# Placing tokens into expert buckets: where GpSimd issues the placements, a third tile table, and how early the first expert tiles start

## The chip, the core and the metric

The kernel runs on one NeuronCore of a Trainium2 chip. Five engines run their own instruction streams and meet only through semaphores: TensorE (PE in the rows), VectorE (DVE), ScalarE (ACT), GpSimd (POOL) and SyncE (SP, which here only issues DMAs). The metric is the device time of one execution in microseconds (us), lower is better. Before the change three runs gave a median of 1045.76 us (1042.63 to 1046.62).

## The reference

x is 16 x 256 x 256 float32, that is 4096 tokens of width 256, or 32 tiles of 128 tokens. The context is 16 x 120 x 256. Four layers follow each other, each with a layernorm in front and a residual behind:

```python
x = x + L0_xattn(layernorm(x), ctx, Wq, Wkv)      # 16 heads of 16
x = x + L0_ffn(layernorm(x), W1, b1, W2, b2, gate_W, shared_W, shared_b, gamma, beta)
x = x + L1_xattn(layernorm(x), ctx, ctx, mask, Wq, Wk, Wv)
x = x + L1_ffn(layernorm(x), weight, bias)        # values rounded to a 6 bit grid

# inside L0_ffn: 8 experts, each token goes to its best two
probs = softmax(flat @ gate_W); topk_w, topk_idx = top_k(probs, 2)
combine = one_hot(topk_idx) * (topk_w / topk_w.sum())
out = 0.5 * gelu(flat @ shared_W + shared_b)
for e in range(8):
    h = gelu(flat @ W1[e] + b1[e])                # 256 -> 1024
    out = out + combine[:, e:e+1] * (h @ W2[e] + b2[e])
out = layernorm(out) * gamma + beta
```

The kernel computes only the two chosen experts of each token. It has to sort tokens by expert for that, and this sorting is what the change is about.

## The kernel before

**Three phases.** `attention_phase` runs the first cross attention and, for every tile, the shared product and the gate's logits. `expert_phase` runs 71 tiles of 128 rows (64 full ones and up to 7 for the remainders of 8 experts); a tile belongs to one expert. `second_phase` does the last two layers; the change does not touch it.

**The order is written out by hand.** Each engine has a function per phase (`sync`, `gpsimd`, `tensor`, `vector`, `scalar`), and what stands first in it runs first. Nothing is reordered, so an instruction that waits holds everything behind it on its engine.

**Attention cycles.** The phase is a loop over 18 cycles b = -2..15, one context batch each, so two token tiles t = 2b and 2b+1. For a tile the vector engine subtracts the row maxima of the scores (`largest`, `less_max`), ScalarE takes exponents, TensorE turns and weighs them, and VectorE divides by the sums (`over_sums`, writes `a_x`). Then GpSimd adds the residual (`residual`, line 757), VectorE takes the statistics (`stats2`, line 1071), GpSimd forms the inverse deviation (`inverse_std2`) and VectorE normalises (`normalise2`). The residual is loaded by SP (`load_residual`, line 622) into `a_xres`, of which there are two; for the even tile it is issued behind two loads of expert weights (`w_sb`, 512 KB each). The key blocks `a_kbd` (`key_blocks`) come once a cycle on GpSimd, so their starts mark off the cycles in the trace.

**Routing.** The 32 tiles form four groups of eight. For a group VectorE picks two experts per token (`choose`, parts 0 to 7, with one exponent on ScalarE), TensorE counts ranks (`count`), and `places` computes each token's row in the buckets. GpSimd then writes token number and weight to that row in HBM: one indirect DMA (`put`, line 405) per tile and choice, 16 per group, 64 in all, 8 bytes per row. `table` computes for each expert tile which expert it has and where its bucket rows start; the first table covers 24 tiles (`EARLY_TILES`) and needs two groups, the second covers the other 47 and needs all four. Groups 0 and 1 are placed in attention cycles 9 to 15, groups 2 and 3 in expert tiles 2 to 5 and 6 to 9.

**Expert tiles.** SP fetches a tile's 128 bucket rows (`slots`, `b_slots`), GpSimd gathers the token rows by them (`gather`, line 1449, four buffers, so three tiles ahead), TensorE turns them (`turn_rows`, line 1504), ScalarE keeps them, TensorE does the first product (`first_product`, line 1515, into `b_H`), ScalarE the gelu, TensorE the second product (line 1527, into `b_Y`), VectorE adds the bias (`finish`, line 1616) and scales by the weight, and GpSimd adds the rows to HBM by an indirect accumulate (`scatter`, line 1460). VectorE also copies the tile's expert weights beforehand (`tile_weights`, `b_w`, line 1605, 1.23 us). In iteration n TensorE runs the first product of tile n+1, turns tile n+2 and runs the second product of tile n. GpSimd's iteration n gathers tile n+3 and then places and scatters; the first scatter is at n = 9. The functions in `starts` let the attention phase begin the first tiles. `gelu_chunk` and `store_chunk` bring the shared part into the accumulator in 16 chunks, all of which must be stored before the first scatter.

## Time and profile before

| | us |
|---|---|
| median of three runs (range) | 1045.76 (1042.63 to 1046.62) |
| the profiled execution's own time | 1037.06 |
| its span in the profile | 1035.3 |
| attention, up to the last attention product that TensorE runs without a gap | about 308 |
| expert tiles, first `b_xT` to last `b_Y` | 317.7 to 866 |
| busy: PE / DVE / ACT / POOL | 946.8 / 529.4 / 509.2 / 515.6 |
| indirect DMAs on POOL: 64 placements, 71 gathers, 71 scatters | 68.1, 75.7, 141.8 busy |

The profiled execution is shorter than the median of the timed runs by 8.7 us; sums over its rows stand against 1037.06. In the page's picture of 40 slices PE is at nine tenths from slice 17 to slice 33, which is most of the expert phase, and between six and nine tenths before. The chain of work that ended last is PE for 44% of the span, nearly all of it the two expert products; "issue" is time in which an engine waited for nothing that the profile shows.

### The profile page before, as it was taken

To read this page: it belongs to the slowest core of one execution; us is meant where nothing else is said; L and a number is where in the kernel's file an instruction comes from. 1 tells how busy PE (TensorE), PEld (TensorE's weight loads), DVE (VectorE), ACT (ScalarE), POOL (GpSimd) and SP (SyncE) were. 2 spreads that over 40 slices of the span, in tenths; PEclk is the share of its full clock that TensorE was granted. 3 is DMA by queue.
4 is the path that set the end of the run, shared out by engine and by line. 5 is a ranking of instruction groups with operands and counts; after the bars stand their busy time and mean duration, and the time that the engine had idled before them with its cause. 6 is when DMAs were issued, how large, how long until landed. Compare 5 with 4: busy or idle time off the path is not lost.

```text
span 1035.3 us, 22010 instructions
## 1 busy us (share of the span) xinstructions
PE 946.8 (91%) x7131; PEld 808.0 (78%) x7131; DVE 529.4 (51%) x1276; ACT 509.2 (49%) x1292; POOL 515.6 (50%) x675
## 2 busy tenths in 40 slices
PE   6999999989876887999999999999999999798776
PEld 4767777666646777899999999999999998676654
DVE  4677898877762332443323232232323223899871
ACT  4776777766643442334333333333333333577663
POOL 2524343655643075656444443434444442688873
PEclk9999999999998998999999999999999999999897
DMA  4264454655643455434322212222121227333210
GB/s 142 81 167 158 133 167 125 154 123 138 158 113 92 151 113 107 36 55 59 51 38 41 37 31 37 34 39 39 34 42 31 42 40 192 111 92 98 86 42 31
DMA packets 90734, 89.58 MB, mean 87 GB/s; under 512 B 19808, under 2 KB 85792, under 8 KB 90496
## 3 DMA queue, kind: packets, MB, share of 16 engines
q1 hardware_dynamic: 74944, 69.48, 23.6%
q0 software_dynamic: 15680, 18.69, 12.3%
q8 instruction: 62, 1.02, 0.5%
q14 instruction: 48, 0.39, 0.2%
HBM read 56.74 MB, written 31.39 MB: 85 GB/s over the span
## 4 chain that ended last, share of the span: by engine, by line
PE 44%; DVE 7%; issue 5%; DMA 3%; POOL 3%; ACT 2%; POOLq 0%; SPq 0%; DVEq 0%; ACTq 0%
PE b_H L1515 20%; PE b_Y L1527 20%; DMA ffn_rows<-b_y,b_slots 2%; POOL buckets L405 2%; DVE c_x_bn L1975 2%; PE c_f_ps L2227 1%; PE b_xT L1504 1%; ACT c_probs L2142 1%; DVE c_centred L1988 1%; ACT c_xn L2097 1%; DVE c_x L2065 1%; DVE c_amax L2045 1%; POOL b_rows L1449 1%; DVE c_nmax L2036 1%; DMA c_ctx<-in_ctx 0%
## 5 line engine op out<-in xcount | busy, mean ns | idle before, releaser
L1684 ACT ACTIVATE b_hiddenT<-b_H,b_b 128x128 f32<-128x128 f32 x568 | 162.5, 369 | 325.5 <-PE b_H L1515 325.5
L1515 PEld LDWEIGHTS b_H<-b_rowsT,b_w 128*128 128x128 f32 x2272 | 266.6, 193 | 4.8 <-ACT b_rowsT L1691 1.1
L1515 PE MATMUL b_H<-b_rowsT,b_w 128*128 128x128 f32 x2272 | 267.4, 276 | 0.5 <-ACT b_rowsT L1691 0.4
L1527 PE MATMUL b_Y<-w_sb,b_hiddenT 128*128 x1136 | 263.0, 386 | 0.0
L1460 POOL DMA_INDIRECT ffn_rows<-b_y,b_slots x71 | 141.8, 1998 | 216.0 <-DVE b_y L1620 141.9
L1527 PEld LDWEIGHTS b_Y<-w_sb,b_hiddenT 128*128 128x128 f32 x1136 | 214.9, 194 | 27.5
L1616 DVE TENSOR_TENSOR b_y<-b_Y,b_b 128x256 f32<-128x256 f32 x71 | 30.1, 425 | 329.9 <-PE b_Y L1527 320.6
L1605 DVE COPY b_w<-w_sb 128x2048 f32 x71 | 87.6, 1234 | 32.2 <-issue 26.0
L1206 ACT COPY a_probsT<-a_T 120x512 f32<-120x512 f32 x128 | 74.9, 585 | 46.6 <-PE a_T L911 40.7
L1449 POOL DMA_INDIRECT b_rows<-xn_rows,b_slots x71 | 75.7, 1066 | 43.2 <-issue 20.8
L405 POOL DMA_INDIRECT buckets<-r_pay,r_place x64 | 68.1, 1064 | 53.9 <-DVE r_place L398 28.6
L911 PE MATMUL a_T<-ident,a_probs 128*120 128x128 f32 x512 | 79.0, 283 | 17.0 <-ACT a_probs L1198 17.0
L911 PEld LDWEIGHTS a_T<-ident,a_probs 128*120 128x120 f32 x512 | 57.3, 140 | 31.6 <-ACT a_probs L1198 20.6
L1198 ACT ACTIVATE a_probs<-a_probs 128x960 f32<-128x960 f32 x64 | 64.3, 1005 | 32.1 <-DVE a_probs L1049 30.8
L757 POOL TENSOR_TENSOR a_x<-a_x,a_xres 128x256 f32<-128x256 f32 x32 | 23.6, 739 | 112.7 <-DMA a_xres<-in_x 57.4
L1041 DVE TENSOR_REDUCE a_max<-a_S 128x8 f32<-128x960 f32 x64 | 73.3, 1146 | 8.9 <-PE a_S L891 8.8
L1049 DVE TENSOR_TENSOR a_probs<-a_S,a_max 128x960 f32<-128x960 f32 x64 | 73.2, 1144 | 0.9 <-issue 0.2
L925 PE MATMUL a_O<-a_probsT,a_vaug 120*32 120x128 f32 x1024 | 54.6, 286 | 0.5 <-ACT a_probsT L1206 0.3
L1504 PE MATMUL b_xT<-ident,b_rows 128*128 128x128 f32 x142 | 28.1, 281 | 20.9 <-DMA b_rows<-xn_rows,b_slots 20.9
L925 PEld LDWEIGHTS a_O<-a_probsT,a_vaug 120*32 120x32 f32 x1024 | 20.2, 108 | 29.4 <-issue 23.0
L2227 PE MATMUL c_f_ps<-c_wdT,c_xdT 128*128 128x256 f32 x128 | 37.7, 448 | 1.4 <-ACT c_xdT L2168 1.4
L1691 ACT COPY b_rowsT<-b_xT 128x256 f32<-128x256 f32 x71 | 27.6, 388 | 21.3 <-PE b_xT L1504 21.3
(222 smaller groups left out, 1315.8 us busy)
## 6 DMA issues: line engine op xcount, KB each, us to landing
w_sb<-in_L_ffn_W SPq DMA_DIRECT2D x32, 512.0 KB, 4.1
a_xin<-in_x SPq DMA_DIRECT2D x16, 256.0 KB, 3.1
a_xres<-in_x SPq DMA_DIRECT2D x32, 128.0 KB, 4.7
x_rows<-a_x SPq DMA_DIRECT2D x32, 128.0 KB, 1.7
xn_rows<-a_xn SPq DMA_DIRECT2D x32, 128.0 KB, 2.7
shared_rows<-a_shared SPq DMA_DIRECT2D x32, 128.0 KB, 2.8
b_spare<-shared_rows SPq DMA_DIRECT2D x16, 256.0 KB, 4.7
ffn_rows<-b_spare SPq DMA_DIRECT2D x16, 256.0 KB, 3.7
```

Of the source, the lines that this page charges most:

```text
L405: pool.indirect_dma_start(bucket_d, IndirectOffsetOnAxis(place[:, t, k:k + 1], 0), pay[:, t, k, :], None).then_inc(s_put[g // 2], 16)
L911: i = pe.transpose(T_ps[q % 2][0:CTX, j * P:(j + 1) * P], pr[q // 2][:, 4 * (q % 2) + j, :], ident[:])
L925: i = pe.matmul(O_ps[VB * j:VB * (j + 1), q * P:(q + 1) * P], vaug[t // 2 % 2][0:CTX, 4 * q + j, :], pT[q % 2][0:CTX, j, :], start=True, s ...
L1041: dve.tensor_reduce(mx[h][:].rearrange("p (r j) -> p r j", r=RG), scores_of(h), AX.X, ALU.max).then_inc(s_mx, 1)
L1049: dve.tensor_tensor(pr[h][:].rearrange("p (r j) c -> p r j c", r=RG), scores_of(h), mx[h][:].rearrange("p (r j) -> p r j", r=RG).unsqueeze ...
L1206: act.copy(pT[q % 2][0:CTX].rearrange("p j n -> p (j n)"), T_ps[q % 2][0:CTX, :]).then_inc(s_T, 1)
L1449: pool.indirect_dma_start(xg[n % AHEAD][:], None, xn2_d, IndirectOffsetOnAxis(iw[:].bitcast(I32)[:, n, 0:1], 0)).then_inc(s_x[n % AHEAD], 16)
L1460: pool.indirect_dma_start(acc_d, IndirectOffsetOnAxis(iw[:].bitcast(I32)[:, n, 0:1], 0), y[n % KEPT_Y][:], None, bounds_check=TOK + SPARE - 1,
L1515: j = pe.matmul(H_ps[i][:, c * P:(c + 1) * P], w1c[i][:, k * HID + c * P:k * HID + (c + 1) * P], xT[:, k * P:(k + 1) * P], start=(k == 0), ...
L1527: j = pe.matmul(y_ps[i][:, 0:D], hT[i][:, c * P:(c + 1) * P], w2_sb[:, bass.ds(e * (HB * D) + c * D, D)], start=(c == 0), stop=(c == HB - 1))
L1605: dve.tensor_copy(w1c[i][:], w1_sb[:, bass.ds(e * (KC * HID), KC * HID)])
L1684: j = act.activation(hT[i][:, c * P:(c + 1) * P], H_ps[i][:, c * P:(c + 1) * P], ACT.Gelu, bias=b1c[i][:, c:c + 1])
```

## The change

It moves instructions in all five streams. Its core, shortened:

```diff
+FIRST_TILES = 9
+    RANGES = ((0, FIRST_TILES), (FIRST_TILES, EARLY_TILES), (EARLY_TILES, SLOT_TILES))
 # GpSimd, attention cycles
-    put_some(b, 1, 1, 2)      # one or two placements at four points of a cycle
...
             for b in CYCLES:
                 t = 2 * b
                 residual(t - 2)
                 add_beta(t - 3)
                 inverse_std2(t - 2)
+                if b == B - 1:
+                    starts["gather"](pool, 0)
+                put_some(b, 3)
+                if 1 <= b < 5:
+                    routing.constants(pool, b - 1)
                 residual(t - 1)
                 add_beta(t - 2)
                 inverse_std2(t - 1)
                 key_blocks(b + 1)
                 inverse_std1(b + 2)
+                put_some(b, 1 if b < FIRST_PUT + 4 else 3 if b == B - 1 else 2)
 # put
+        if g % 2 == 1 and (t % GT, k) == (0, 0):
+            pool.wait_ge(s_put[g // 2], 16 * 2 * GT)
 # SyncE, attention cycles
-                if b == 2:
-                    routing.fill_buckets(sp)
+                if 4 <= b < 7:
+                    routing.fill_buckets(sp, b - 4)
...
-            starts["slots"](sp, 0)
+                if b == B - 2:
+                    starts["slots"](sp, 0)
+                if b == B - 1:
+                    starts["load_b2"](sp)
+                    starts["slots"](sp, 1)
             load_residual(TILES - 1)
-            starts["slots"](sp, 1)
 # TensorE, end of the attention phase
+                if b == B - 1:
+                    starts["rows"](pe, 0)
                 turn_probs(t + 1, 2)
...
             weigh(t, 2)
+            starts["first"](pe, 0, 0)
             weigh(t, 3)
             shared_gate(t - 2)
+            starts["first"](pe, 0, 1)
             pe.wait_ge(s_oT, TILES)
             turn_back(t)
-            starts["rows"](pe, 0)
             turn_xn2(t - 1)
-            starts["first"](pe, 0, 0)
+            starts["rows"](pe, 1)
             shared_gate(t - 1)
-            starts["first"](pe, 0, 1)
-            starts["rows"](pe, 1)
+            starts["first"](pe, 1, 0)
+            starts["first"](pe, 1, 1)
+            starts["rows"](pe, 2)
             turn_xn2(t)
-            starts["first"](pe, 1, 0)
+            starts["second"](pe, 0)
             shared_gate(t)
-            starts["first"](pe, 1, 1)
 # VectorE, end of the attention phase
                 less_max(t + 1, 1)
+                if b == B - 1:
+                    starts["weights"](dve, 0)
                 keep_shared(t - 2)
...
             normalise2(t - 1)
-            starts["weights"](dve, 0)
             over_sums(t)
             stats2(t)
+            starts["weights"](dve, 1)
             keep_shared(t - 1)
-            starts["weights"](dve, 1)
             normalise2(t)
+            routing.table(dve, 1, 3)
+            starts["weights"](dve, 2)
             keep_shared(t)
+            starts["finish"](dve, 0)
 # expert phase
-        CONST_AT = 10
+        CONST_AT = 11
-        COUNT_AT = {1: THIRD, 5: LAST}
-        PUT_AT = {2: THIRD, 6: LAST}
-        TABLE_AT = 7
+        COUNT_AT = {5: THIRD, 9: LAST}
+        PLACE_AT = {5: THIRD, 9: LAST}
+        PUT_AT = {6: THIRD, 10: LAST}
+        TABLE_AT = 10
+        EXTRA_ADD = 16
-                return 0 if n < FIRST_ADD else 2 if (n - FIRST_ADD) % 4 == 0 else 1
+                return 0 if n < FIRST_ADD else 2 if n >= EXTRA_ADD and n % 4 == 0 else 1
-            for s, value in past["attention"] + past["rows_stored"]:
-                sp.wait_ge(s, value)
-            sp.dma_start(b2_bc[:], b2.rearrange("e d -> (e d)").partition_broadcast(P)
-                         ).then_inc(s_b12, 16)
```

In words: the first 16 placements of tokens (group 0) alone now decide a first table of nine tiles, the next 15 tiles get a table from groups 0 and 1, and the last 47 one from all groups. The attention phase now contains the whole of tile 0 and the first products of tile 1. The second bias (`b2`, 1 MB once it is broadcast over the partitions) is loaded in the last attention cycle and has memory of its own there. Groups 2 and 3 are chosen and counted later, and placed at tiles 6 to 9 and 10 to 13. GpSimd's constants are made in four parts in cycles 1 to 4 instead of at once in cycle 1, and the initial filling of buckets, spare rows and accumulator is issued in cycles 4, 5 and 6 instead of in cycle 2. The turned rows of tiles 0 and 1 go to a part of `b_H`'s memory.

GpSimd's stream in attention cycle 13 before. L757 is `residual`, L766 `add_beta`, L405 a placement, L747 and L750 `inverse_std2`, L775 `key_blocks`, L735 to L741 `inverse_std1`:

```order
L757 TENSOR_TENSOR a_x_0<-a_x_0,a_xres 128x256
L766 TENSOR_TENSOR a_x_1<-a_x_1,a_beta 128x256
L405 DMA buckets<-r_pay,r_place 32896x2
L747 TENSOR_SCALAR a_var_eps<-a_mv 128x1
L750 TENSOR_TENSOR a_rstd<-a_var_eps,a_minus_half 128x1
L757 TENSOR_TENSOR a_x_1<-a_x_1,a_xres 128x256
L766 TENSOR_TENSOR a_x_0<-a_x_0,a_beta 128x256
L405 DMA buckets<-r_pay,r_place 32896x2 x2
```

The same stretch of the same cycle in the changed kernel, where the lines are 781, 790, 420, 771 and 774:

```order
L781 TENSOR_TENSOR a_x_0<-a_x_0,a_xres 128x256
L790 TENSOR_TENSOR a_x_1<-a_x_1,a_beta 128x256
L771 TENSOR_SCALAR a_var_eps<-a_mv 128x1
L774 TENSOR_TENSOR a_rstd<-a_var_eps,a_minus_half 128x1
L420 DMA buckets<-r_pay,r_place 32896x2 x3
L781 TENSOR_TENSOR a_x_1<-a_x_1,a_xres 128x256
L790 TENSOR_TENSOR a_x_0<-a_x_0,a_beta 128x256
```

The placement that stood ahead of `inverse_std2` now stands behind it with two more, between the even tile's residual and the odd tile's; those behind the odd tile's go to the cycle's end.

GpSimd in attention cycle 15, changed kernel (before, no gather stood in the cycle; the first one came behind the residual of tile 30). L1489 is the gather:

```order
L771 TENSOR_SCALAR a_var_eps<-a_mv 128x1
L774 TENSOR_TENSOR a_rstd<-a_var_eps,a_minus_half 128x1
L1489 DMA b_rows<-xn_rows,b_slots 128x256
L420 DMA buckets<-r_pay,r_place 32896x2 x3
L781 TENSOR_TENSOR a_x_1<-a_x_1,a_xres 128x256
```

The gather of tile 0, which waits for its bucket rows (`b_slots`), now stands ahead of the residual of tile 29.

SyncE at the turn from cycle 14 to cycle 15, before. L1394 loads a chunk, L622 a residual, L629 stores `a_x`, L650 loads expert weights:

```order
L1394 DMA b_spare<-shared_rows 128x2x256
L622 DMA a_xres<-in_x 128x256
L629 DMA x_rows<-a_x_0 128x256
L650 DMA w_sb<-in_L_ffn_W 128x1024
```

and in the changed kernel, where four tiles' bucket rows (L1408 reads a row number, L1409 issues the load; one of the four is shown) stand in between:

```order
L1436 DMA b_spare<-shared_rows 128x2x256
L1408 TENSOR_LOAD r_tile_row
L1408 ISA x2
L1409 ISA
L1409 DMA b_slots<-buckets 128x2
```

Behind the fourth of these comes the residual load of tile 29, which before followed the chunk's load directly.

## Rows read from the trace of the kernel before

**Rows 1.** Windows: stretch, length, busy of PE, PEld, DVE, ACT, POOL; clock, DMA.

```profile
440.60:855.90 415.30, 415.30 (x2865) 391.55 (x2864) 124.18 (x237) 146.43 (x515) 187.59 (x120) 1.00 0.26 42
335.33:440.60 105.27, 88.88 (x579) 81.58 (x578) 37.99 (x113) 39.13 (x116) 53.88 (x46) 0.92 0.49 100
164.49:281.50 117.01, 107.38 (x1073) 78.05 (x1072) 91.83 (x208) 79.96 (x141) 67.70 (x110) 0.99 0.56 141
113.52:146.97 33.45, 33.45 (x349) 25.12 (x348) 30.07 (x67) 26.19 (x48) 13.82 (x29) 1.00 0.46 149
41.04:79.19 38.15, 35.65 (x353) 25.54 (x353) 27.11 (x54) 26.15 (x46) 17.61 (x48) 1.00 0.55 157
```

**Rows 2.** Waits of DVE, 113.52 to 146.97: total us, times, longest.

```profile
DVE a_bn L1071 <- POOL a_x L757: 1.2, 2, 0.6
```

**Rows 3.** Waits of DVE, 164.49 to 281.50.

```profile
DVE a_bn L1071 <- POOL a_x L757: 19.9, 8, 4.3
```

**Rows 4.** Timeline of POOL, cycle 13: start, us, line, what [idle before <-releaser].

```profile
243.99 1.07 POOL L405 DMA_INDIRECT buckets<-r_pay,r_place  x1 [0.56 <-issue]
246.72 0.72 POOL L757 TENSOR_TENSOR a_x<-a_x,a_xres 128x256 f32<-128x256 f32 x1 [1.66 <-DMA a_xres<-in_x]
255.87 0.73 POOL L757 TENSOR_TENSOR a_x<-a_x,a_xres 128x256 f32<-128x256 f32 x1 [5.64 <-DMA a_xres<-in_x]
```

**Rows 5.** Tile a_xres, 113.52 to 164.49: landing times of the residual loads.

```profile
DMA to landing us min/median/max: 2.6/3.6/5.0
```

**Rows 6.** Tile a_xres, 164.49 to 281.50: landing times.

```profile
DMA to landing us min/median/max: 3.3/5.1/7.4
```

**Rows 7.** Timeline of SP's DMA queue, 289 to 313 us.

```profile
290.40 0.49 SPq L622 DMA_DIRECT2D a_xres<-in_x  x1
...
308.94 3.69 SPq L1373 DMA_DIRECT2D b_slots<-buckets  x4
312.68 0.43 SPq L622 DMA_DIRECT2D a_xres<-in_x  x1
```

**Rows 8.** Timeline of POOL, 296 to 316 us.

```profile
296.88 0.72 POOL L757 TENSOR_TENSOR a_x<-a_x,a_xres 128x256 f32<-128x256 f32 x1 [5.58 <-DVE a_x L1062]
...
314.81 1.09 POOL L1449 DMA_INDIRECT b_rows<-xn_rows,b_slots  x1 [7.71 <-DMA b_slots<-buckets]
```

**Rows 9.** Timeline of PE, 317 to 409 us.

```profile
317.68 0.69 PE L1504 MATMUL b_xT<-ident,b_rows 128*128 128x128 f32 x2 [9.16 <-DMA b_rows<-xn_rows,b_slots]
...
335.33 3.73 PE L1515 MATMUL b_H<-b_rowsT,b_w 128*128 128x128 f32 x32
...
343.89 0.22 PE L381 MATMUL b_pre<-r_sel,r_before 128*128 128x72 bf16 x1 [4.61 <-DVE r_sel L353]
...
370.70 0.67 PE L1504 MATMUL b_xT<-ident,b_rows 128*128 128x128 f32 x2 [3.39 <-DMA b_rows<-xn_rows,b_slots]
...
408.09 0.69 PE L1504 MATMUL b_xT<-ident,b_rows 128*128 128x128 f32 x2 [5.65 <-DMA b_rows<-xn_rows,b_slots]
```

**Rows 10.** Timeline of POOL, 379 to 431 us.

```profile
379.60 1.83 POOL L405 DMA_INDIRECT buckets<-r_pay,r_place  x1 [0.30 <-issue]
...
395.39 1.81 POOL L405 DMA_INDIRECT buckets<-r_pay,r_place  x1 [7.98 <-DVE r_pay L358]
...
401.32 1.79 POOL L1449 DMA_INDIRECT b_rows<-xn_rows,b_slots  x1 [0.30 <-issue]
...
414.91 0.98 POOL L1449 DMA_INDIRECT b_rows<-xn_rows,b_slots  x1 [0.30 <-issue]
...
428.94 0.99 POOL L405 DMA_INDIRECT buckets<-r_pay,r_place  x1 [0.30 <-issue]
430.23 0.98 POOL L1449 DMA_INDIRECT b_rows<-xn_rows,b_slots  x1 [0.30 <-issue]
```

**Rows 11.** Waits of SP, 400 to 440 us.

```profile
SPq L1370 <- DMA buckets<-r_pay,r_place: 1.6, 1, 1.6
```

**Rows 12.** Timeline of DVE, 341 us.

```profile
341.44 0.42 DVE L1616 TENSOR_TENSOR b_y<-b_Y,b_b 128x256 f32<-128x256 f32 x1 [9.31 <-DMA b_b<-in_L_ffn_b]
```

322 lines of the change are left out of this document (175 added, 147 removed).

## The prediction

> **What bounds the kernel now.** I read the windows first [rows 1]. From 440.6 us on the expert phase is TensorE's alone: it is busy for the whole window, 57 tiles in 415.3 us, so 7.29 us a tile with the few extra products in it. That floor stays. The time is lost in front of it. The eleven tiles between 335.3 and 440.6 us took 105.3 us where 11 x 7.29 = 80.1 would do: 25.2 us lost, 16.4 of them idle TensorE (105.3 less 88.9 busy), the rest mostly a granted clock of 0.92, since TensorE falls back to its lower level, 1.2 of 2.4 GHz, after each gap. In the attention phase I took the stretches between key block operations as cycles. Cycles 6 and 7 take 16.7 us each (33.45 for two) with TensorE busy throughout; cycles 9 to 14, in which groups 0 and 1 are placed, take 117.0, 16.7 more than six times that.
>
> The views of waits say why. In the undisturbed cycles VectorE waits 1.2 us for the residual that GpSimd adds [rows 2], in the six others 19.9 us in eight waits [rows 3]. But GpSimd is not simply busy with placements: in cycle 13 one ends at 245.1 and the even tile's residual starts at 246.72, released by the residual's load, and the odd tile's waits for its load as well [rows 4]. These loads land after 3.6 us (median) without placements about [rows 5] and after 5.1, up to 7.4, with them [rows 6]. So a placement costs twice: 1.3 us of GpSimd (0.99 + 0.30), and slower transfers around it.
>
> The timeline of TensorE between 317 and 409 us gives the gaps in the expert phase [rows 9]: 9.2 us before the first tile (gather), 4.6 us for the third group's selection, 3.4 and 5.7 us for gathers. Behind the 4.6 stands VectorE, which had waited 9.3 us for the second bias [rows 12]. Behind the 5.7 stands GpSimd, which waited 8.0 us with a placement whose weights were not ready, while the gather queued behind it, issued at 401.3, reached TensorE at 408.1 [rows 10].
>
> **The change part by part.** Sums are over the profiled execution (1037.06 us for a span of 1035.3; 8.7 under the median of 1045.76) and are then taken off the median.
>
> *Constants and filling.* The two cycles from 41.0 to 79.2 us took 38.15 [rows 1], 4.7 over two undisturbed ones. In them GpSimd made its constants in one piece, and the filling of buckets and spare rows stood ahead of a residual load. In four parts behind `inverse_std2` the constants lie in an idle stretch of GpSimd; the filling still stands in SP's queue, now in three cycles. I take 1.5 us gained. Ends: 0 (each part costs what the whole did) and 4.7.
>
> *Placements in the attention cycles.* Their number stays: 4 in cycles 9 to 12 as before, then 5, 5 and 6 for 6, 6 and 4. Three now stand after `inverse_std2` of the even tile, ahead of a residual for which GpSimd waits 5.6 us anyway [rows 4]: 3 x 1.3 = 3.9 fits. The three that lay between the odd and the next even residual shrink to one (two in 13 and 14). The even residual then comes with the load, about 1.5 to 2.5 us sooner a cycle. The bill goes to the odd tile: its load is now in flight beside three placements, and if it lands after 5.1 rather than 3.6 it is late by up to 1.5. VectorE cannot go below the 16.7 us cycle. So 17.6 us for each of cycles 9 to 12 (before, 18.75 on average in them), 19.5 for 13 and 14, which also carry chunk loads and one new wait: the first placement of group 1 waits until all of group 0 have landed. How long a placement takes to land can be bounded: the last one started at 428.94, and SP waited 1.6 us for it [rows 11] from the table's end at 432.1, so 4.8 us. That is 4 x 17.6 + 2 x 19.5 = 109.4, 7.6 less than 117.0; I take 6, since in that count nothing goes wrong. Ends: a loss of 4 (odd tiles late by 1.5 and the even ones no sooner: 6 x 1.5 = 9 lost against 5 gained) and a gain of 14 (nearly all the excess).
>
> *Cycle 15 and the turn into the expert phase.* Here I expect no gain, against what three early tiles suggest. The bucket rows of tiles 0 to 3 are issued at the end of SP's cycle 14, where before the residual load stood at 290.4 [rows 7]. Four take 3.7 us, so until 294.1, and before the gather began 2.2 us after their last issue (312.63, 314.81 [rows 7, 8]): 296.3 now. GpSimd stands at that gather from about 289, and behind it are queued three placements and the residual of tile 29: 296.3 + 1.4 + 3.9 gives 301.6 instead of 296.9 [rows 8]. VectorE needs that residual before it can subtract the next maxima, so the last two tiles are 4.7 us late. VectorE's copy of tile 0's weights, 1.4 us with its bias, now stands ahead of the gate's read on which TensorE waits, and the first two halves of the first product (3.6 us) stand ahead of the last turns: TensorE ends the attention products near 318 rather than 308.5. SP then has the bias and five more rows, 0.4 + 4.6 us, ahead of the residual load of tile 31, which was issued at 312.7 [rows 7] and will be at about 317.5, landing 3.6 later, 321. Statistics and the weight copy of tile 1 follow: its first product starts at about 324.4. Two halves (3.9), two turns (0.8), the second product of tile 0 (3.5), a gate product (1.1) and 1.5 of low clock bring the next tile's first product to 335.2, as before (335.33 [rows 9]). The 9.2 us gap is filled and comes back as two smaller ones. I take 0. Ends: +5 (load of tile 31 hidden) and -5 (both delays longer).
>
> *Tiles 1 to 11.* The bias is there, so the 4.6 us gap goes, and no placement waits for weights in tiles 2 to 9, since groups 2 and 3 are chosen three tiles ahead of their placing. What is late next is GpSimd in tiles 6 to 13, where placements and scatters now lie together for five tiles (9 to 13) instead of one. Two iterations of four placements and a gather took 414.91 - 401.32 = 13.6 us [rows 10], 6.8 each, which fits into 7.29. A scatter is 2.0 us busy on average and 0.3 between: 9.15 an iteration. From the start of tile 6's iteration on TensorE: placements begin after VectorE's places, at 2.7, and end at 8.2; two iterations make 21.9; five with a scatter 67.7; and the first placement of group 3 waits for the landing of group 2's last, 4.8 less what lies between, 2.5 more: the gather of tile 17 is issued at 70.2. It lands after 2.9 (314.81 to 317.68 [rows 8, 9]) to 6.8 us (401.32 to 408.09); with 4.8, 75.0. TensorE wants it at 9 x 7.29 + 3.8 = 69.4. So 5.6 us late, and 2 for the low clock after a gap (8.8 us of excess over busy and idle time before, for four gaps): 7.5 lost. Gain 25.2 - 7.5 = 17.7. Ends: 25 (a scatter hides between placements and landings are short) and 9 (every iteration meets a weight copy).
>
> That last end rests on a row: placements and gathers that fall beside VectorE's weight copy took 1.8 us, three in the rows, others 0.98 [rows 10], 0.85 more. The Trainium skill (SBUF — State Buffer, "Who interferes with whom") says that a VectorE copy in its two-port mode takes the shared port pair for the whole instruction, and that GpSimd's descriptor writing is fully blocked meanwhile; so every tile would charge GpSimd up to the copy's length. The trace agrees in kind, with 0.85. The page's rule speaks against this change, as the copies come once a tile: at 0.85 in each of eight iterations, against one in two in the 6.8, it would be 3.4 us more lateness, and the forecast would be 1024.
>
> *Choosing, counting and tables later.* VectorE is busy 124 of 415 us in the expert phase [rows 1]; the 0.2 us steps and the third table hide there. If they did not, the cost were under 3 us. TensorE's counts are the same instructions.
>
> Sum: 1.5 + 6 + 0 + 17.7 = 25.2 us; 1037.1 - 25.2 = 1011.9, and of the median 1045.8 - 25.2 = 1020.6.
>
> **The rivals.** *B, all goes well*: attention cycles near their floor and GpSimd never late: 3 + 9 + 1 + 23 = 36, 1010. For it: 5.6 us idle before the odd residual. Against: slower landings beside placements.
>
> *C, the lateness moves*: the odd tile's load takes what the even one's gives, and tiles 12 to 15 wait longer for gathers: 0 + 0 + 0 + 12, 1034. For it: the odd residual too waited for its load in cycle 13 [rows 4].
>
> *D, the early tiles cost what the later ones give*: the delay in cycle 15 is twice mine (-9), tiles gain 12, attention nothing: 3 us, 1043. For it: five things queue behind one gather. Against: 25 us were lost before in a place that the change clears.
>
> *E, slower, one mechanism*: placements slow other transfers wherever they stand. The iteration of tile 9 before had four placements, a gather and two scatters and took 430.23 - 414.91 = 15.3 us [rows 10]. If the five iterations with one scatter take that, the gather of tile 17 starts at 21.9 + 76.5 = 98.4 and is 33.8 us late; with 2 of clock 35.8 are lost against 25.2 before, and the attention cycles gain nothing: 1045.8 - 1.5 + 10.6 = 1055. It decides for slower from about 14.5 us an iteration. Against: that iteration held the wait of the second scatter for the first, which one a tile does not have.
>
> **How the numbers follow.** Forecast 1020.5, own range 1014 to 1029, chance 0.50; B 0.15; C 0.20; D 0.09; E 0.06. A difference of 0.5%, 5.2 us, is about what a measurement of this kernel can tell from none. Faster by more holds the forecast, B, C and a little of D: 0.87; within it 0.08 (D); slower 0.05 (E, less its edge). The range 1010 to 1036 takes in B's and C's values and leaves out D and E and half of B's tail.
>
> **What would show it.** Right: cycles 9 to 14 together 105 to 114 us; VectorE's wait for the residual under 12 us there; in cycle 15 a wait of GpSimd for bucket rows at the first gather and VectorE idle 4 to 5 us behind it; no TensorE gap over 1 us in tiles 1 to 8; gaps for gathered rows between tiles 11 and 16, 4 to 8 us in sum. Wrong: residual waits unchanged in sum (C), a GpSimd iteration over 12 us in tiles 9 to 13 (E), TensorE's first product of tile 2 after 340 us on the new clock of the trace (D), or gaps in tiles 1 to 5, which I price at nothing.

## The result, and the profile after

| | before | changed | ratio, 95% interval |
|---|---|---|---|
| timed, median (range) | 1045.76 us (1042.63 to 1046.62) | 1027.98 us (1025.12 to 1036.61) | 0.9869 (0.9838 to 0.9899) |
| a second set of runs | 1046.08 us (1039.82 to 1048.64) | 1029.86 us (1024.37 to 1032.96) | 0.9849 (0.9793 to 0.9904) |
| profiled executions | 1037.06, 1040.56 us | 1036.61, 1027.53 us | |

The first row stands on five executions of each kernel, the second on seven of before and four of the changed one. A ratio leaves out executions that lie over 1.5% above the fastest of their kernel, which are three in experiment 7 and one in experiment 8. The change makes the kernel 14 to 18 us faster; 25.2 were forecast. The first profiled execution of before is shorter than all its timed ones and the first of the changed kernel is its longest, so this pair alone would show nothing (0.4 us). I therefore use two profiles of each, and the experiments' where they leave a stretch as it is. Below, *mark n* is the n-th start of a key block operation, counted from 0 (41.04 us of before is mark 2; what the prediction calls cycles 9 to 14 lies between marks 9 and 15), and *tile n* the start of tile n's first product. These stretches come from the traces' instruction starts.

| stretch, us | before | changed | forecast of the gain | gain of the means |
|---|---|---|---|---|
| start to mark 9 | 164.5, 163.4 | 159.7, 160.4 | 1.5 | 3.9 |
| mark 9 to 15 | 117.0, 115.2 | 117.8, 107.5 | 6 | 3.5 |
| mark 15 to tile 2 | 53.8, 52.3 | 61.5, 59.9 | 0 | -7.6 |
| tile 2 to 13 | 105.3, 118.9 | 98.7, 98.1 | 17.7, less what tiles 13 to 16 lose | 13.7 |
| tile 13 to 24 | 81.9, 81.9 | 87.8, 92.2 | (in the row above) | -8.1 |
| tile 24 to 70 | 333.3, 333.3 | 333.3, 333.3 | 0 | 0 |
| tile 70 to the end | 179.6, 173.9 | 176.1, 174.5 | 0 | 1.4 |

Rows two and three need care, for the change moved mark 15 itself. Before, two placements stood between the residual of tile 27 and the key blocks; now they stand behind. GpSimd, before and then changed (first profiles):

```profile
276.64 0.73 POOL L757 TENSOR_TENSOR a_x<-a_x,a_xres 128x256 f32<-128x256 f32 x1 [5.58 <-DMA a_xres<-in_x]
281.50 1.24 POOL L775 TENSOR_TENSOR a_kbd<-a_kT,a_head_mask 128x240 f32<-128x240 f32 x2
```

```profile
275.17 0.72 POOL L781 TENSOR_TENSOR a_x<-a_x,a_xres 128x256 f32<-128x256 f32 x1 [6.18 <-DMA a_xres<-in_x]
277.51 1.12 POOL L799 TENSOR_TENSOR a_kbd<-a_kT,a_head_mask 128x240 f32<-128x240 f32 x2
```

The mark follows that residual by 4.8 to 4.9 us in all profiles with the old placement points and by 2.3 to 2.5 in all with the new, so 2.4 us change rows without any time being won or lost (mark 9 has not moved). From the residual of tile 15 to that of tile 27 the kernel before took 114.6 and 112.8 us and the changed one 117.9 and 107.5, a gain of 1.0; from there to tile 2 it is 58.7 and 57.2 against 63.9 and 62.3, a loss of 5.2.

The windows of the changed kernel that answer to [rows 1] (length, busy time of PE, PEld, DVE, ACT and POOL, clock, DMA share, GB/s). First profile; the stretches are mark 9 to 15, tile 2 to 13 and tile 13 to 16:

```profile
159.73:277.51 117.78, 106.56 (x1068) 77.19 (x1066) 90.37 (x210) 77.97 (x139) 66.10 (x109) 0.99 0.49 135
339.04:437.70 98.66, 88.85 (x576) 81.48 (x575) 35.10 (x107) 41.58 (x120) 35.77 (x32) 0.91 0.41 98
437.70:466.90 29.20, 25.66 (x163) 21.94 (x161) 13.29 (x36) 8.52 (x29) 22.41 (x18) 1.00 0.41 38
```

Second profile, the same three:

```profile
160.35:267.90 107.55, 103.71 (x1056) 75.10 (x1054) 90.00 (x211) 78.19 (x139) 65.99 (x110) 1.00 0.52 148
327.80:425.90 98.10, 86.93 (x577) 80.36 (x575) 35.10 (x107) 41.90 (x120) 35.65 (x32) 0.91 0.42 99
425.90:459.70 33.80, 28.25 (x164) 23.51 (x163) 13.47 (x35) 8.63 (x29) 25.34 (x21) 0.95 0.38 40
```

In the attention cycles VectorE's wait for the residual, 19.9 us before [rows 3], and GpSimd's wait for the residual's input stand thus in the first profile:

```profile
DVE a_bn L1097 <- POOL a_x L781: 18.4, 10, 4.6
POOL a_x L781 <- DMA a_xres<-in_x: 30.9, 8, 6.5
```

and in the second:

```profile
DVE a_bn L1097 <- POOL a_x L781: 11.9, 9, 2.3
POOL a_x L781 <- DMA a_xres<-in_x: 14.5, 7, 3.9
```

The same instructions, once with half the waiting: the placements' order did not settle this. What did is not found.

Cycle 15, first profile. GpSimd, answering to [rows 8]:

```profile
296.80 1.08 POOL L1489 DMA_INDIRECT b_rows<-xn_rows,b_slots  x1 [9.34 <-DMA b_slots<-buckets]
...
301.78 0.73 POOL L781 TENSOR_TENSOR a_x<-a_x,a_xres 128x256 f32<-128x256 f32 x1
...
314.32 0.82 POOL L781 TENSOR_TENSOR a_x<-a_x,a_xres 128x256 f32<-128x256 f32 x1 [6.32 <-DVE a_x L1088]
...
325.59 0.72 POOL L781 TENSOR_TENSOR a_x<-a_x,a_xres 128x256 f32<-128x256 f32 x1 [7.54 <-DMA a_xres<-in_x]
```

SP's queue, answering to [rows 7]:

```profile
290.57 4.06 SPq L1409 DMA_DIRECT2D b_slots<-buckets  x4
294.67 0.43 SPq L643 DMA_DIRECT2D a_xres<-in_x  x1
...
303.59 0.43 SPq L671 DMA_DIRECT2D w_sb<-in_L_ffn_W  x1
...
317.24 0.39 SPq L1427 DMA_DIRECT2D b_b<-in_L_ffn_b  x1
318.48 4.77 SPq L1409 DMA_DIRECT2D b_slots<-buckets  x5
323.30 0.43 SPq L643 DMA_DIRECT2D a_xres<-in_x  x1
```

VectorE's copy of tile 0's weights:

```profile
310.47 1.23 DVE L1650 COPY b_w<-w_sb 128x2048 f32 x1 [3.97 <-issue]
```

and TensorE, answering to [rows 9]:

```profile
305.34 1.11 PE L934 MATMUL a_T<-ident,a_probs 128*120 128x128 f32 x4 [8.10 <-ACT a_probs L1226]
312.32 1.09 PE L960 MATMUL a_M<-ident,a_oT 128*128 128x128 f32 x4 [5.87 <-DVE logits L1122]
...
329.00 5.42 PE L1562 MATMUL b_H<-b_rowsT,b_w 128*128 128x128 f32 x32 [3.21 <-DVE b_b L1651]
...
339.04 3.73 PE L1562 MATMUL b_H<-b_rowsT,b_w 128*128 128x128 f32 x32
```

The gather at 296.80 and the residual at 301.78 were forecast at 296.3 and 301.6. But the prediction counted on the clock of the trace before. Counted from the residual of tile 27 (276.64 before, 275.17 here, 265.37 in the second profile), the residual of tile 29 was forecast at 25.0 us, and came at 26.6 and 24.9. The rest is worse than forecast: the input of tile 31 was to be asked for 15.9 us behind that residual and was asked for 21.5 and 21.7 us behind it.

The chain between the two is in the rows. The store of tile 28's `a_x` waits for GpSimd's work behind the late residual, and the last load of the first product's weights stands behind this store in SP's queue: issued at 303.6 (298.7 before). VectorE's copy of tile 0's weights waits in the code for all 16 of these loads (`s_w1`). The profile calls this wait of 3.97 us "issue", but the trace has the last landing at 309.4 and the copy at 310.5. The gate's read stands behind the copy, TensorE waits 5.87 us for it, GpSimd's residual of tile 30 waits 6.32 us for VectorE, and only then does SP come to its stores, the bias, the five slots and the input of tile 31. The second profile has the same wait, 4.14 us. Tile 1's first product starts at 329.0 instead of 324.4.

In the expert phase VectorE's 9.3 us wait for the second bias [rows 12] is gone:

```profile
340.07 0.42 DVE L1663 TENSOR_TENSOR b_y<-b_Y,b_b 128x256 f32<-128x256 f32 x1 [0.34 <-issue]
```

The 4.6 us gap for the selection and the gathers' gaps in tiles 1 to 7 are gone (tile 3 to 8 took 36.6 us in both profiles; 42.4 and 55.0 before). Then this happens, in both, at tile 9. TensorE, second profile:

```profile
380.92 4.90 PE L1562 MATMUL b_H<-b_rowsT,b_w 128*128 128x128 f32 x25 [2.00 <-issue]
386.95 0.39 PE L1562 MATMUL b_H<-b_rowsT,b_w 128*128 128x128 f32 x2 [1.13 <-issue]
387.68 0.27 PE L1562 MATMUL b_H<-b_rowsT,b_w 128*128 128x128 f32 x1 [0.34 <-issue]
389.10 0.57 PE L1562 MATMUL b_H<-b_rowsT,b_w 128*128 128x128 f32 x1 [1.15 <-issue]
391.22 0.37 PE L1562 MATMUL b_H<-b_rowsT,b_w 128*128 128x128 f32 x1 [1.55 <-issue]
393.36 0.37 PE L1562 MATMUL b_H<-b_rowsT,b_w 128*128 128x128 f32 x1 [1.77 <-issue]
...
396.23 0.37 PE L1551 MATMUL b_xT<-ident,b_rows 128*128 128x128 f32 x1 [1.76 <-issue]
```

GpSimd meanwhile, unhindered:

```profile
387.54 0.98 POOL L420 DMA_INDIRECT buckets<-r_pay,r_place  x1 [0.30 <-issue]
...
390.10 1.62 POOL L1500 DMA_INDIRECT ffn_rows<-b_y,b_slots  x1 [0.30 <-issue]
```

A product of 32 matmuls that takes 3.73 us elsewhere takes 13.5 (380.92 to 394.47). Most single matmuls last 0.27 to 0.39 us but start 0.7, 1.4 or 2.1 us apart, and no release is named ("issue"): in these rows TensorE waits for no other engine and for no data that the profile knows. Tile 8 to 13 took 54.8 and 54.3 us where the pitch gives 36.5. I call this the crawl. The granted clock is lower there: 0.91 over the window above.

The other engines stand too. In the first profile, where the same happens at tile 9:

```profile
386.65 3.62 PE L1583 MATMUL b_Y<-w_sb,b_hiddenT 128*128 x16
394.78 6.08 PE L1562 MATMUL b_H<-b_rowsT,b_w 128*128 128x128 f32 x25 [4.51 <-ACT b_rowsT L1739]
```

```profile
393.32 1.14 ACT L1732 ACTIVATE b_hiddenT<-b_H,b_b 128x128 f32<-128x128 f32 x4 [6.90 <-remote]
406.90 0.42 DVE L1663 TENSOR_TENSOR b_y<-b_Y,b_b 128x256 f32<-128x256 f32 x1 [19.35 <-remote]
```

By TensorE's row the second product ends at 390.3. The trace has the semaphore update that VectorE waits for at 406.8, 16.5 us later; in the second profile the corresponding update comes 14.4 us behind its row. One tile earlier both stand at 383.0. So the crawl is not only late starts of TensorE: results that its rows show as finished are signalled late.

### The profile page after: what moved, and what is told of

The parts are those of the page before. It is cut to its first block, busy times and chain, and to the rows that moved or that the text cites. A ratio compares the mean times of both kernels' runs of the same rounds, so it can differ in the third digit from the quotient of the medians.

```text
span 1034.9 us, 22048 instructions
## 1 busy us (share of the span) xinstructions
PE 944.5 (91%) x7131; PEld 805.1 (78%) x7131; DVE 532.5 (51%) x1300; ACT 509.8 (49%) x1294; POOL 512.5 (50%) x675
## 4 chain that ended last, share of the span: by engine, by line
PE 68%; DVE 9%; DMA 8%; issue 4%; ACT 4%; POOL 3%; SPq 3%; another core or an unknown queue 1%; DVEq 0%; POOLq 0%; ACTq 0%
PE b_H L1562 24%; PE b_Y L1583 23%; DMA a_xres<-in_x 4%; PE a_T L934 4%; PE a_O L889 3%; PE a_O L948 3%; PE a_S L914 2%; DVE c_x_bn L2023 2%; DMA ffn_rows<-b_y,b_slots 2%; PE b_xT L1551 1%; PE a_M L983 1%; ACT c_xn L2145 1%; ACT c_probs L2190 1%; DVE c_centred L2036 1%; PE a_M L960 1%
## 5 line engine op out<-in xcount | busy, mean ns | idle before, releaser
L1562 PEld LDWEIGHTS b_H<-b_rowsT,b_w 128*128 128x128 f32 x2272 | 269.6, 195 | 20.7 <-issue 10.1
L1562 PE MATMUL b_H<-b_rowsT,b_w 128*128 128x128 f32 x2272 | 272.2, 278 | 13.9 <-ACT b_rowsT L1739 6.0
L1583 PE MATMUL b_Y<-w_sb,b_hiddenT 128*128 x1136 | 260.3, 382 | 1.5 <-issue 1.3
L1583 PEld LDWEIGHTS b_Y<-w_sb,b_hiddenT 128*128 128x128 f32 x1136 | 212.1, 192 | 29.1 <-issue 2.8
L1500 POOL DMA_INDIRECT ffn_rows<-b_y,b_slots x71 | 137.6, 1938 | 190.1 <-DVE b_y L1667 124.7
L1489 POOL DMA_INDIRECT b_rows<-xn_rows,b_slots x71 | 78.0, 1099 | 72.7 <-PE b_xT L1551 45.6
L934 PEld LDWEIGHTS a_T<-ident,a_probs 128*120 128x120 f32 x512 | 58.3, 141 | 35.2 <-ACT a_probs L1226 24.6
L948 PE MATMUL a_O<-a_probsT,a_vaug 120*32 120x128 f32 x1024 | 54.3, 285 | 0.4 <-ACT a_probsT L1234 0.3
L948 PEld LDWEIGHTS a_O<-a_probsT,a_vaug 120*32 120x32 f32 x1024 | 20.2, 108 | 28.9 <-issue 22.7
L983 PE MATMUL a_M<-a_wsg,a_xn2T 128*128 128x264 f32 x128 | 35.6, 401 | 0.2 <-ACT a_xn2T L1249 0.2
L914 PE MATMUL a_S<-a_kbd,a_qT 32*128 32x240 f32 x512 | 35.0, 387 | 0.9 <-ACT a_qT L1210 0.8
L2275 PE MATMUL c_f_ps<-c_wdT,c_xdT 128*128 128x256 f32 x128 | 33.7, 411 | 1.4 <-ACT c_xdT L2216 1.4
```

The costliest lines, as they stand in the source:

```text
L934: i = pe.transpose(T_ps[q % 2][0:CTX, j * P:(j + 1) * P], pr[q // 2][:, 4 * (q % 2) + j, :], ident[:])
L948: i = pe.matmul(O_ps[VB * j:VB * (j + 1), q * P:(q + 1) * P], vaug[t // 2 % 2][0:CTX, 4 * q + j, :], pT[q % 2][0:CTX, j, :], start=True, s ...
L1489: pool.indirect_dma_start(xg[n % AHEAD][:], None, xn2_d, IndirectOffsetOnAxis(iw[:].bitcast(I32)[:, n, 0:1], 0)).then_inc(s_x[n % AHEAD], 16)
L1500: pool.indirect_dma_start(acc_d, IndirectOffsetOnAxis(iw[:].bitcast(I32)[:, n, 0:1], 0), y[n % KEPT_Y][:], None, bounds_check=TOK + SPARE - 1,
L1562: j = pe.matmul(H_ps[i][:, c * P:(c + 1) * P], w1c[i][:, k * HID + c * P:k * HID + (c + 1) * P], xT[:, k * P:(k + 1) * P], start=(k == 0), ...
L1583: j = pe.matmul(y_ps[i][:, 0:D], hT[i][:, c * P:(c + 1) * P], w2_sb[:, bass.ds(e * (HB * D) + c * D, D)], start=(c == 0), stop=(c == HB - 1))
```

## The experiments

All are edits of the changed kernel unless another base is named. Ratios are to the kernel before, run beside them. Experiments 1 to 3 ran on one chip, 4 to 7 on a second, 8 to 10 on a third and 11 on a fourth. Each edited kernel has one profile.

**1. Both kernels again.**

> The changed kernel once more, nothing edited. Time: 1024 to 1031 by its five runs (median 1027.98). Theory T1 (the stretch from 390 to 410 us of the profiled execution, in which ScalarE waited 6.9 and 13.4 us and VectorE 19.4 us for a release that the profile calls remote, belongs to that one execution, the slowest of its five): it is missing here or elsewhere, the execution is 5 to 12 us shorter than 1036.6, and the stretch from the first product of tile 2 to that of tile 13 takes 84 to 92 us instead of 98.7. Rival (it belongs to the order of the work, as the third group's placements run beside chunk stores there): it is back in the same iteration and the stretch takes 96 to 101 us again. Placements in attention: both theories expect 116 to 119 us again for the cycles from mark 9 to mark 15.

> The kernel before once more, nothing edited, for a second profile. Its five runs lie 6 to 9 us above the profiled execution. If profiled executions are simply as long as timed ones and the first was a short one, this one takes 1042 to 1047 us, and the profile shows where the 6 to 9 us more lie; if profiling shortens this kernel, it is again at 1036 to 1038.

Measured: the changed kernel 1029.86 us, profile 1027.53; its crawl is back in the same tile, so the rival holds and T1 falls. Mark 9 to 15 took 107.5 us instead of the 116 to 119 that I expected from either. Before: profile 1040.56 us, again in the lower part of its runs (1039.8 to 1048.6). It has a crawl of its own at tile 5, which the first profile of before has not:

```profile
373.31 0.69 PE L1504 MATMUL b_xT<-ident,b_rows 128*128 128x128 f32 x2 [8.96 <-issue]
```

Where the timed runs of before spend 5 to 9 us more than its profiles stays open.

**2. Cycle 15.**

```diff
 (SP)      load_residual(t - 1)
+          if b == B - 1: starts["slots"](sp, 0)      # was: end of cycle 14
...
           store_shared(t - 3)
+          if b == B - 1: load_residual(TILES - 1)    # was: behind slots 1
           store_xn2(t - 1)
 (GpSimd)  inverse_std2(t - 2)
-          if b == B - 1: starts["gather"](pool, 0)
           put_some(b, 3)
...
           residual(t - 1); add_beta(t - 2); inverse_std2(t - 1)
+          if b == B - 1: starts["gather"](pool, 0)
```

> Only the last cycle of attention is edited: the first slots are asked for after the residual input of tile 29, the residual input of tile 31 ahead of the last stores and of the second slots, and the first gather stands behind the residual addition of tile 29 on GpSimd. Theory T2 (the forecast put the gather 9 us late at no cost, and missed that the input of tile 31 was now queued behind nine slots: together the first product of tile 2 came 3.7 us later than before instead of level): 4 to 9 us faster than the changed kernel, 1019 to 1024, with the first product of tile 2 at some 333 instead of 339. Rival (the turn is bound by TensorE's own order there, the waits stand beside it): within 2 us of 1028, and the waits at the residual additions are gone without effect. Second rival (the gather now comes too late for the first product of tile 0): 1030 to 1036.

Measured: 1018.67 us, ratio 0.9741 (0.9691 to 0.9791), 11 to 13 us faster than the changed kernel; mark 15 to tile 2 took 49.7 us instead of 61.5 and 59.9. T2 holds, and its price was more than I gave it. The edit moves three things at once, and no run here parts them. The last weight load is issued 20.2 us behind the residual of tile 27 (28.4 and 26.8 in the changed kernel), VectorE's copy waits half as long, and TensorE's first product of tile 1 waits 1.33 instead of 3.21 us for that tile's weight and bias copy:

```profile
287.04 0.43 SPq L671 DMA_DIRECT2D w_sb<-in_L_ffn_W  x1
```

```profile
291.89 1.23 DVE L1651 COPY b_w<-w_sb 128x2048 f32 x1 [1.95 <-issue]
```

```profile
309.73 3.81 PE L1563 MATMUL b_H<-b_rowsT,b_w 128*128 128x128 f32 x32 [1.33 <-DVE b_b L1652]
```

**3. Placements at their old points.** `put_some(b, 1, 1, 2)`, `(1, 2, 1)`, `(1, 1, 1)`, `(1, 2, 0)` at the four places of before, instead of three behind `inverse_std2(t - 2)` and the rest at the cycle's end.

> The placements of the first 32 columns stand where they stood before (between the normalisations' parts, one to two at four points of a cycle), all else is as in the changed kernel. Theory T3 (moving them did nothing: the cycles from mark 9 to 15 took 117.8 us against 117.0, because the even residuals' waits for GpSimd were traded for waits of the odd ones for the residual's input): within 3 us of 1028, 1025 to 1031, cycles 9 to 15 at 116 to 120 us. Rival (the placements' new points do save the 6 us forecast, and something else in the changed kernel, as the fillings' new cycles, gives them back): 1032 to 1037, these cycles at 122 to 126 us.

Measured: 1022.31 us, ratio 0.9786 (0.9743 to 0.9828), 7 us *faster* than with the new points, which neither side expected. Mark 9 to 15 took 114.4 us; mark 15 to tile 2 took 52.6. From the residual of tile 27 to tile 2 it took 57.4 us against 63.9 and 62.3. The new points do not lose in the cycles but in the last one: it now holds six placements (four before), three of them between the gather and tile 29's residual.

**4. Both edits together.**

> Both edits together: the last cycle's order of the first experiment on it, and the placements of the first two groups at their old points. If the two cure different things, they add: 1029.9 less 11.2 less 7.5, so 1011. If both do no more than free the last cycle (six placements and a gather around two residual additions, in the changed kernel; four placements in the old arrangement), they overlap: 1017 to 1021. If the old points cost in the cycles before, as the profiles have it (mark 9 to 15 took 114.4 us with them and 107.5 and 109.1 without): 1018 to 1024.

Measured: 1018.03 us, ratio 0.9751 (0.9683 to 0.9818): no better than experiment 2 alone. Mark 15 to tile 2 fell to 47.2 us and mark 9 to 15 took 116.3, but 2.4 us of both are the mark's own shift: from the residual of tile 27 to tile 2 it is 52.1 us, in experiment 2 52.2. They overlap fully. With the last cycle in order, the placement points of the first two groups are worth nothing that these runs can tell.

**5. Without the late placements.** `PUT_AT = {}`; groups 2 and 3 never reach their buckets, so half of the routed work is missing from the output.

> The changed kernel without the 32 placements of the third and fourth group in the expert phase: they are left out, and the slots from tile 24 on are read from the buckets' filling, so half of the routed work is missing from the output, while the work of every tile is issued as before. Tiles 8 to 16 (first product to first product) took 84 us in one profile of the changed kernel and 88 in the other, where the pitch of the later tiles, 7.3 us, gives 58.5; in both, TensorE's matmuls stand 0.7 to 2 us apart for some 15 us beside the placements, with no wait that the profile can name. Theory T4 (the placements cause it, by what their many small packets do to the delivery of something else, as instructions): the stretch falls to 59 to 64 us, and the time to 1003 to 1010. Rival T5 (the stores and loads of 256 KB beside them cause it, the shared rows' and the second layer's weights): the stretch stays at 75 to 88 us, and the time falls only by the placements' own lateness on GpSimd, to 1018 to 1026.

Measured: 1006.75 us, ratio 0.9649 (0.9597 to 0.9701), 21 to 23 us faster than the changed kernel. Tile 8 to 13, which took 54.8 and 54.3 us, now (windows view, columns as above):

```profile
382.60:419.60 37.00, 37.00 (x266) 34.92 (x265) 15.85 (x47) 14.88 (x49) 16.02 (x11) 1.00 0.44 106
```

TensorE is never idle; tile 8 to 16 took 61.3 us. T4 holds in so far as this profile has no crawl without placements, and all four executions are faster than any of the changed kernel; the stores and loads beside them were all there.

**6. The second layer's weights later.** `sp.wait_ge(routing.s_put[1], all)` ahead of the four loads, `CONST_AT = 20`.

> The changed kernel with the four loads of the second layer's weights (256 KB each) held back until the last placement has landed, and with the work on these weights nine tiles later, in the body. T5 in its narrow form (these four loads, issued at 388 us in the second profile of the changed kernel, hold up the delivery of instructions): the stretch from tile 8 to 16 falls from 84 to 88 us to 65 to 72, the time to 1008 to 1016. T4 (the placements alone do it) and T5 by the stores before these loads: the stretch stays at 80 to 88, the time at 1025 to 1031.

Measured: 1021.28 us, ratio 0.9779 (0.9713 to 0.9845). The crawl stays (tile 8 to 13 took 50.8 us), so these loads do not cause it; tile 13 to 16 takes 25.5 us instead of 29.3 and 33.8, where a part of the gain lies. The gain of 7 to 9 us lies at the edge of the intervals. The sum came out between the two theories.

**7. Constants and fillings as before** (one piece in cycle 1, four fillings in cycle 2).

> The changed kernel with the constants in one piece at the end of cycle 1 and all four fillings in cycle 2, as before. The profiles gave this part of the change 5 us up to mark 4 (79.2 and 79.5 before, 73.8 and 74.5 behind), of which 1.5 are given back between mark 6 and 9, where the fillings now stand. Theory T6 (it is worth 4 to 6 us, not the 1.5 forecast): 1032 to 1036, mark 4 at 78 to 80. Rival (as forecast, 1 to 2 us, and the rest comes from elsewhere): 1029 to 1032.

Measured: 1032.37 us, ratio 0.9882 (0.9845 to 0.9919), 1.4 to 3.5 us slower than the changed kernel, so nearer the rival by time, and within the intervals. The profiled execution, 1040.46 us, is one of the three left out of the ratio, so I read only its start: mark 4 comes at 79.7 us (73.8 and 74.4 in the changed kernel; 73.8 to 74.7 in all profiles with the new constants and fillings, 79.2 and 79.5 before), and mark 9 at 163.9 (159.7 and 160.4). Some 4 us is my reading: 5.5 gained, 1.7 given back up to mark 9.

**8. Experiments 2 and 6 together.**

> The last cycle's order of the first experiment on it, together with the second layer's weight loads held back behind the last placement. They touch different stretches, so they should add: as ratios to the kernel before 0.9741 and 0.9779 against 0.986 for the changed kernel, hence 0.966, 1010. In the profile: mark 15 to the first product of tile 2 in some 50 us (49.7 and 47.2 with that order so far, 59 to 62 without), tiles 8 to 16 in 76 to 80 us. If the weights' gain was chance (the spread of the runs is 10 us): 0.974 again, 1018.

Measured: 1002.82 us, ratio 0.9647 (0.9600 to 0.9694), as the sum of both had it. But the profile shows what I had not expected, tile 8 to 13 and 13 to 24:

```profile
360.80:397.40 36.60, 36.60 (x262) 34.52 (x261) 15.64 (x47) 13.91 (x47) 26.08 (x23) 1.00 0.46 60
397.40:487.80 90.40, 84.17 (x568) 77.72 (x567) 28.96 (x63) 29.89 (x102) 57.30 (x42) 1.00 0.45 60
```

No crawl, with the same placements in the same tiles as in experiment 6, which crawled. The two differ by the last cycle's order, which did not keep experiments 2 and 4 from crawling, and by the chip. Whether the one profile without a crawl is the kernel's, the chip's or chance is not known. With it out of the way GpSimd's lateness shows as forecast, TensorE waiting for gathered rows at four tiles, the longest wait:

```profile
403.01 0.44 PE L1553 MATMUL b_xT<-ident,b_rows 128*128 128x128 f32 x2 [1.75 <-DMA b_rows<-xn_rows,b_slots]
```

and on GpSimd a tile of four placements and a gather in 7.0 us, one placement of it longer, and the wait for the third group's landing:

```profile
369.26 0.99 POOL L1491 DMA_INDIRECT b_rows<-xn_rows,b_slots  x1 [0.30 <-issue]
370.56 0.98 POOL L420 DMA_INDIRECT buckets<-r_pay,r_place  x1 [0.30 <-issue]
371.85 1.56 POOL L420 DMA_INDIRECT buckets<-r_pay,r_place  x1 [0.30 <-issue]
...
376.27 0.99 POOL L1491 DMA_INDIRECT b_rows<-xn_rows,b_slots  x1 [0.30 <-issue]
...
389.93 0.98 POOL L420 DMA_INDIRECT buckets<-r_pay,r_place  x1 [3.78 <-DMA buckets<-r_pay,r_place]
```

**9. Late placements four tiles later** (`PUT_AT = {10: THIRD, 14: LAST}`, `CONST_AT = 24`), on experiment 8.

> The kernel of the run before it in this set, with the placements of the third and fourth group four tiles later, 10 to 17 instead of 6 to 13, clear of the 256 KB stores and loads of the shared rows, which end near tile 9. Theory T4 (the placements by themselves hold up what TensorE is to execute): the 15 to 25 us are lost again, now between tiles 12 and 20: tiles 8 to 16 and 16 to 24 together take 130 to 140 us, and the time is that of its base, 1008 to 1014. Rival T7 (only placements beside bulk stores do it): these 16 tiles take 117 to 124 us, and it is 12 to 18 us faster than its base, 993 to 1000.

Measured: 1010.87 us, ratio 0.9759 (0.9715 to 0.9803), so 11 us slower than its base. No crawl (tile 8 to 16 took 58.3 us, and no such rows stand up to tile 24), against T4 in its plain form, though its base had no crawl to lose either; but the gathers come late further on (tile 16 to 24 took 70.1 us), one by this much:

```profile
452.74 0.69 PE L1553 MATMUL b_xT<-ident,b_rows 128*128 128x128 f32 x2 [5.71 <-DMA b_rows<-xn_rows,b_slots]
```

In that profile the 16 tiles took 128.4 us, under T4's 130 to 140 and over the rival's 124. The rival's 993 to 1000 missed as well.

**10. Late placements spread**, three a tile over tiles 6 to 16, on experiment 8 with `CONST_AT = 24`.

> The same base with the 32 late placements spread thinner: three a tile over tiles 6 to 16 instead of four over 6 to 13. If each placement costs TensorE a fixed amount wherever it stands (some 25 us over 32 of them, 0.8 us each): as its base, 1008 to 1014, tiles 8 to 24 at 130 to 140 us. If the loss comes from GpSimd's queue being full (four placements, a gather and a scatter take 7.7 of a tile's 7.3 us, at 1.28 us each), three a tile leave 1.2 us of air and the loss falls by half or more: 995 to 1003.

Measured: 1001.82 us, ratio 0.9661 (0.9622 to 0.9701): as its base. No crawl, as in its base; one wait for gathered rows, 2.8 us. Tile 8 to 24 took 121.7 us against the base's 127.0, but tile 24 to 40 119.0 against 116.4, with the constants later. The base itself lost little here, so my first theory's fixed 25 us falls and the second has little left to save.

**11. The residual's input ahead of the weights**, on experiment 10.

```diff
-                load_expert_weights(b)
                 load_residual(t)
+                load_expert_weights(b)
```

> The kernel with the late placements spread (the last cycle's order, weights later, three late placements a tile), and one edit more: in every cycle of attention the residual input of the even tile is asked for ahead of the cycle's expert weights (two loads of 512 KB) instead of behind them. Theory T8 (what decides the attention cycles 9 to 15 is how long GpSimd waits for that input: 14.5, 21.2 and 23.3 us of such waits in the profiles where they took 107.5, 108.5 and 111.5 us, and 30.9 to 33.9 us where they took 117 to 122, with either set of placement points): the waits fall below 10 us, the cycles 9 to 15 take 100 to 107 us, the earlier cycles (17.4 us each between marks 6 and 9) gain up to 1 us each, and the time is 6 to 14 us below its base: 0.953 to 0.961 of the kernel before, against 0.966. Rival (the weights, issued up to 3 us later, then delay the other residual input or the next batch's by as much): 0.963 to 0.970, the waits only change places.

Measured: 997.54 us, but the kernel before took 1027.12 beside it: ratio 0.9689 (0.9654 to 0.9725), no gain over experiment 10. T8 fails. GpSimd's waits for the input fell from 9 to 5 in number and hardly in sum:

```profile
POOL a_x L782 <- DMA a_xres<-in_x: 19.5, 5, 5.8
```

So the two 512 KB loads ahead of the input are not what makes it late; the rival (the waits change places) fits. The lowest ratios of all are those of experiments 8 and 10, 0.965 and 0.966, not to be told apart.

## Why the prediction was right, and where not

*The sign and the range* held: 1028 and 1030 for 1020.5, in 1010 to 1036; of its own range, 1014 to 1029, the first lies inside and the second 0.9 us outside. The way there was in good part another: the constants gave more than forecast, the placements, the turn and the tiles less. A cost that was in no term, the crawl, is as large as the whole gain, so that the total stayed in the range is in part luck. Of the signs, the absence of gaps over 1 us holds from tile 2 to tile 8, while tile 1's first product waited 3.21; VectorE's wait for the residual was 18.4 and 11.9 us where under 12 was the sign.

*Constants and filling*: 1.5 forecast, some 4 measured (profiles, experiment 7). Right mechanism, mis-sized: I thought the fillings would cost in SP's queue what they cost before, but of some 5 us gained up to mark 4, only 1.3 to 1.7 are given back.

*Placements in the attention cycles*: 109.4 us forecast, 6 taken. Eight profiles with the new points (those of the changed kernel and of experiments 2, 5, 6, 8, 9 and 10) took 107.5, 108.5, 108.9, 109.1, 111.5 and 117.3, 117.8, 119.7 us; four with the old points 114.4 to 117.0. Left out are experiment 7 (121.9, one of its longest executions) and experiment 11 (110.0, other order of loads). The mean gain is 3.2 us, but 2.4 of it is the shift of mark 15: between the two residuals, 112.6 us with the new points and 113.3 with the old, it is 0.7. This step failed as a sum, and rival C's outcome, no gain there, is the nearer one. GpSimd's waits for the residual's input go with the length: 14.5 to 23.3 us in the five executions up to 111.5, 26.9 to 32.6 in the three from 117.3. What sets them apart is not found. The median landing of the loads does not sort them (5.2 us in experiment 9 at 108.9, 4.0 in experiment 3 at 114.4), and experiment 11 excludes the weights ahead of them in the queue. In cycle 15 the new points cost more than they give: with them at their old places the changed kernel is 7 us faster (experiment 3), and with the last cycle cured the points make no difference (experiment 4 against 2).

*Cycle 15 and the turn*: 0 forecast, ends plus and minus 5; measured 7.6 lost from mark 15, 5.2 from the residual of tile 27. This step failed. The queueing was right within 2 us up to the residual of tile 29. The failed term is VectorE's copy of tile 0's weights, priced at 1.4 us: it also waits 4.0 and 4.1 us for the landing of the last expert weights, whose load the late residual had held back in SP's queue. So the input of tile 31 was asked for 5.6 and 5.8 us later behind that residual than the prediction had it; on it the statistics and the weight copy of tile 1 hang. Experiment 2, by order alone, brought 10 to 12 us back in that stretch. That three early tiles give nothing there was right; they need not have cost anything.

*Tiles 1 to 11*: 17.7 forecast (7.5 lost in place of 25.2), ends 9 and 25. Tile 2 to 24 took 186.4 and 190.3 us against 187.1 and 200.8 before, 5.6 less in the mean. This step failed too, and not by its own mechanism: where there is no crawl (experiment 8) a tile of placements takes GpSimd 7.0 us (6.8 forecast), the wait for landing is 3.8 (2.5), waits for gathered rows are 4.5 in sum (4 to 8), and tile 2 to 24 takes 170.9 us, 11 over the pitch of 7.25. The crawl costs 13 to 18 us more in tiles 8 to 13 alone (50.0 to 54.8 us against 36.6) and was in no term. It was readable in kind from nothing that I used: the first profile of before has no such rows. On the rule of the Trainium skill (SBUF — State Buffer, "Who interferes with whom"), the trace agrees in direction again: in experiment 8 one placement a tile takes 1.5 to 1.6 us instead of 0.98, 0.6 more, less than the 0.85 of [rows 10]. By its size the rule's 1024 lay nearer the result than 1020.5, but not for its reason.

*Rivals*: B's expert phase is experiment 5's; C's first half, no gain in the attention cycles, is what the mean of the executions shows; D's loss of 9 in the turn was not met (5.2, or 7.6 by the mark); E's 15.3 us an iteration did not come.

*What is shown and what is not.* Shown: the turn's loss is a matter of order. Supported, but on one profile and four executions: without the late placements there is no crawl, and they cost at least as much as the change brings (experiment 5, on a chip on which experiments 4, 6 and 7 crawled). The crawl stood in seven of the eight profiles with four placements a tile over tiles 6 to 13, not in experiment 8's. It did not stand in experiments 9, 10 and 11 either, with fewer a tile or with them later, but all three are built on experiment 8 and ran on its chip or a fourth one, so they do not show that spreading or moving the placements cures it. To part these, experiment 8's kernel and the changed one would have to be profiled several times on one chip.

Not shown: what the crawl is. For a shortage of instructions speaks that TensorE starts single matmuls on a grid of 0.7 us with no release named, and that its large instruction packets (16 KB) come 28 to 32 us apart around the crawl instead of some 13 to 20. Against it, these packets number ten in tiles 2 to 24 with the crawl and without, so their pace may just follow TensorE; and the late semaphore updates of products whose rows had ended are not explained by it. Also open: the timed gain is 16 to 18 us by medians, that of the profiles' means 6.8.

## What to carry to other kernels

Work brought forward into a last stage must not stand ahead of what the stage's own end hangs on: write down, for each in-order queue, the load that the last tile needs, and put nothing before it that only the next phase needs. Moving small scattered transfers into an engine's idle time pays for the engine's time alone; what they do beside others has to be looked for in every execution, so take two or three profiles before explaining some microseconds. Measure a stretch between instructions that the change does not reorder: here the mark itself moved by 2.4 us, most of what the cycles seemed to gain. And where two parts of a change overlap at one place (here placements and a gather in the last cycle), test them together as well as alone.
